# Holding GpSimd's indirect DMAs back so that at most two are queued

## The reference

```python
h = layernorm(x)
agg_in  = segment_mean((h @ W_in.T  + b_in )[src], dst)
agg_out = segment_mean((h @ W_out.T + b_out)[dst], src)
gi = concat([agg_in, agg_out]) @ W_ih.T + b_ih
gh = h @ W_hh.T + b_hh
r = sigmoid(i_r + h_r);  z = sigmoid(i_i + h_i)
n = tanh(i_n + r * h_n)
x = x + (1 - z) * h + z * n
f = layernorm(x)
p = softmax(relu(f @ router_w1 + router_b1) @ router_w2 + router_b2)
top_w, top_i = top_k(p, 2);  w = softmax(top_w)
x = x + sum(w * expert_out[top_i])      # 6 experts of three 256x256 layers
```

## Time and profile before

| | us |
|---|---|
| timed runs, median of 3 (lowest to highest) | 3107.05 (3097.07 to 3108.61) |
| the profiled execution: its span | 4434.5 |
| first scatter of GpSimd starts at | 114.68 |
| first gather of direction 0 starts at | 940.15 |
| first gather of direction 1 starts at | 2302.12 |
| first gather of the experts starts at | 4035.59 |

### The profile page before, as it was taken

How to read it: one execution, slowest core, us unless ns; L and a number is a source line. 1 busy time by engine, 2 the same in 40 slices (tenths; PEclk the granted TensorE clock), 3 DMA queues, 4 the chain that set the end, 5 groups by cost and what they waited for, 6 DMA issues and landing times. The chain is left out here.

```text
span 4434.5 us, 68226 instructions
## 1 busy us (share of the span) xinstructions
PE 2745.1 (62%) x14312; PEld 1616.8 (36%) x14313; DVE 2093.1 (47%) x6910; ACT 908.1 (20%) x1572; POOL 2164.5 (49%) x2165
## 2 busy tenths in 40 slices
PE   5211159977777777777764555555555555566896
PEld 2100025533333333333322333333333333345775
DVE  8201179975565556655552333443333433354221
ACT  4100026631112111111110010110111101112443
POOL 0777700035665555655645444444444444433786
PEclk9655589988888888888877777777777777787998
DMA  3100000022222222222222222222222222212444
GB/s 116 30 24 24 18 16 0 0 95 80 86 81 82 78 79 81 79 83 81 84 72 83 77 82 72 74 79 74 83 72 76 75 75 82 71 60 45 80 80 61
DMA packets 178175, 298.24 MB, mean 67 GB/s; under 512 B 51779, under 2 KB 123460, under 8 KB 178118
## 3 DMA queue, kind: packets, MB, share of 16 engines
q0 software_dynamic: 106560, 234.06, 19.8%
q10 hardware_dynamic: 44790, 35.90, 2.6%
q1 hardware_dynamic: 26768, 27.70, 2.0%
HBM read 255.56 MB, written 41.94 MB: 67 GB/s over the span
## 5 line engine op out<-in xcount | busy, mean ns | idle before, releaser
L431 POOL DMA_INDIRECT ring<-split_rows,live x782 | 791.5, 1012 | 923.4 <-DVE live L1035 381.8
L431 POOL DMA_INDIRECT over<-split_rows,gather_row x782 | 747.5, 956 | 933.0 <-PE bank L1674 681.5
L1600 PE MATMUL bank<-over,over 128*128 (+1 forms) x4920 | 1008.9, 354 | 143.1 <-issue 123.6
L1600 PEld LDWEIGHTS bank<-over,over 128*128 (+1 forms) x4920 | 485.9, 102 | 597.7 <-issue 351.9
L974 DVE TENSOR_SCALAR over<-iota_cols,live,live 128x128 f16 x1564 | 411.4, 319 | 119.9 <-issue 113.1
L392 POOL DMA_INDIRECT list<-sort,sort x336 | 332.7, 990 | 218.3 <-issue 111.0
L1674 PE MATMUL bank<-ring,dense 128*128 x980 | 329.5, 430 | 126.7 <-issue 100.1
L1714 PE MATMUL bank<-dense,dense 128*128 128x512 f32 (+1 forms) x600 | 262.0, 437 | 184.5 <-DVE dense L1183 174.1
L1675 PE MATMUL bank<-ones_col,dense 128*128 128x1 f16 x1960 | 334.9, 171 | 2.7 <-issue 2.5
L1674 PE MATMUL bank<-over,dense 128*128 x980 | 277.7, 386 | 94.5 <-issue 77.8
L614 ACT ACTIVATE over<-live,live 128x788 f16 x245 | 221.6, 945 | 492.2 <-remote 271.7
(11 more groups left out here) (304 smaller groups left out, 3927.7 us busy)
## 6 DMA issues: line engine op xcount, KB each, us to landing
norm<-in_x SPq DMA_DIRECT2D x20, 640.0 KB
ring<-split_rows,live POOLq DMA_INDIRECT x782
over<-split_rows,gather_row POOLq DMA_INDIRECT x782
split_rows<-over SPq DMA_DIRECT2D x10, 640.0 KB
in_edge_means<-dense ACTq DMA_DIRECT2D x50, 128.0 KB
dense<-in_x ACTq DMA_DIRECT2D x50, 128.0 KB
dense<-in_edge_means ACTq DMA_DIRECT2D x50, 128.0 KB
out<-dense ACTq DMA_DIRECT2D x25, 256.0 KB
```

Of the source, the lines that this page charges most:

```text
L431: g.indirect_dma_start(out=rings[d][:, i % ring_slots[d], :], out_offset=None, in_=table[:], in_offset=bass.IndirectOffsetOnAxis(ap=gather ...
L1600: ins = t.matmul(bank[h][:, 0:HS + 1], rows_(half), slots(h), start=False, stop=False, skip_group_check=True)
```

## The change

Ahead of each of the 2,116 indirect DMAs GpSimd's program gets a wait, and each of these DMAs gets a second semaphore, `sent`, which is raised when the DMA has left the engine (not when its rows have landed; the semaphores for that stay as they are). The wait ahead of the n-th DMA asks that `sent` stands at n - 2, so that at any time two indirect DMAs at most are with the engine. Nothing else is touched.

```diff
+SENT_AHEAD = 2
...
-        names = ("consts const_step spread_ready ...
+        names = ("sent consts const_step spread_ready ...
...
         @block.gpsimd
         def _(pool):
             g = nc.gpsimd
+            issued = [0]
+
+            def few_queued():
+                issued[0] += 1
+                if issued[0] > SENT_AHEAD:
+                    pool.wait_ge(S["sent"], issued[0] - SENT_AHEAD)
...
             for t_ in range(SORTED_TILES, NS):
+                few_queued()
                 g.indirect_dma_start(
                     out=lists[0][:], out_offset=bass.IndirectOffsetOnAxis(ap=list_at[:, t_:t_ + 1], axis=0),
-                    in_=payload[:, 0, t_:t_ + 1], in_offset=None,
+                    in_=payload[:, 0, t_:t_ + 1], in_offset=None, engine_sem=S["sent"],
                 ).then_inc(scatter_landed, 16)
...
                     if i % BATCH == 0 and i >= ring_slots[d]:
                         pool.wait_ge(S["slot_done"], d * NS + i + BATCH - ring_slots[d])
+                    few_queued()
                     g.indirect_dma_start(
                         out=rings[d][:, i % ring_slots[d], :], out_offset=None, in_=table[:],
                         in_offset=bass.IndirectOffsetOnAxis(ap=gather_row[d][:, i:i + 1], axis=0),
+                        engine_sem=S["sent"],
                     ).then_inc(ring_landed[d][i // BATCH % (ring_slots[d] // BATCH)], 16)
```

More of the change, by code:

```diff
@@ L297, in gnn_moe_program @@
         place_at = sb("place_at", [P, 2, 4], F32)
-        names = ("consts const_step spread_ready edges_in ln_mean ln_stats rows_scaled h_ready hi_ready split_ready table_stored "
+        names = ("sent consts const_step spread_ready edges_in ln_mean ln_stats rows_scaled h_ready hi_ready split_ready table_stored "
                  "dve_step onehot_ready onehot_used slots16_ready slot_prefix_ready base_ready "
```

## The result

The median of 20 timed runs after the change is 3114.80 us, of 20 runs before it 3102.32; the ratio, with one execution left out (below), is 1.0033, with a 95% interval of 1.0020 to 1.0046. The change costs some 10 us of 3100: within the half per cent that the prediction called no change and within its range, but clear of zero, and on the other side of zero than its 3105 (3107 - 2).

What follows compares the result with a forecast made beforehand. GpSimd's stream of indirect DMAs was taken as the bound. Median 3107 less a gain of 2, with wait, instructions and queued work at cost 0, gave 3105 us; range of this case 3085 to 3125, whole range 2990 to 3190.

Steps and rivals of the forecast that it cites:

- The stream is the bound: GpSimd's indirect DMAs, 1.25 to 1.32 us a step, already pace the timed runs; nothing else binds.
- chain without late signals: Whole kernel: GpSimd's scatters, gathers of both directions, stretches between and experts sum to 3082 us, timed median 25 above.
- TensorE was further from binding than feared: Gather stages: TensorE's 992 and 890 us lie under the stream's 1026 and 982, only 34 to spare in direction 0.
- Late signals a property of the profiled execution almost alone: TensorE's semaphores: lateness makes up the profile's 1353 us excess over 3082, hardly any of it in timed runs.
- "Cost 0" of the wait, with DMA n-1 as cover: Ahead of each indirect DMA: the 0.27 us release hides behind DMA n-1 with 0.98 us to spare; cost 0.
- The range of that term: Wait ahead of the 2,116 DMAs: bounds 0 and 571 us, the upper with DMAs served one at a time.
- The added instructions: A wait and semaphore more per DMA: bounds 0 and 127 us, taken as 0 from gathers already carrying a `slot_done` wait.
- A, the hold does nothing: Rival: queue not the cause, or `sent` raised on handing over; profile near 4430, timed 3107 us; chance 0.17.
- B, late signals in timed runs: Rival, faster: timed steps 0.82 us, TensorE binds after the change; 2919 us, or 3000 with half the lateness; chance 0.20.
- C, slower: Rival: hold not hidden, `sent` late or some ns per DMA; 10 ns make +21 us, 60 ns +127; chance 0.23.
- The gain of 2 us: Timed runs: of at most 25 us that the median has above the chain, the change removes 2.

Runs made afterwards that it cites:

- one execution left out (below): One of the 20 timed executions of the changed kernel, no further edit: 4257.33 us at a mean granted TensorE clock of 0.735.
- the earlier trace: The unchanged kernel as profiled ahead of the prediction: 4434.5 us at a mean granted TensorE clock of 0.808.

## Why the prediction was right and wrong

**The stream is the bound: right.** The prediction's chain without late signals came to 3082 us; the trace of the kernel before, taken again, spans 3092.5, that of the change 3100.1. Stage by stage, prediction and kernel before again: first gather 566 and 573.8, direction 0 1026 and 1021.4, direction 1 982 and 1010.4, experts' first gather 2683 and 2690.4. Of these, only direction 1 is off by more than 10 us: its gathers took 956 ns on average in the earlier trace rows and 986 here, which is 24 us. The stretches between the directions and ahead of the experts give 11 and 12 back (17.5 us for 28.8, 67 for 79), so that the total comes within 0.3% is in part luck. TensorE was further from binding than feared: 834 us in direction 0, not 992, with a granted clock of 0.98 there and not 0.85; the kernel before, taken again, has 837 us at 0.98.

**"Late signals a property of the profiled execution almost alone": right about timed runs, wrong about what they belong to.** The kernel before, profiled again, has none. The prediction saw that 4434.5 and 3107 do not belong together, and drew the right consequence, that the timed runs had nothing to give back. It took the wrong cause, and so credited the change with emptying the profile of "remote" waits and bringing the span to 3080 to 3200. The span did come to 3100.1, and the waits are gone, but the unchanged kernel does the same. Whether the hold would shorten an execution like that of the earlier trace rows is open, as no trace shows one with the hold.

**"Cost 0" of the wait, with DMA n-1 as cover: the step that failed.** As far as it went, it was right: `sent` comes 0.010 us after a DMA's end, the cover of 0.98 us is there, and the gathers start 0.30 us after the one before as ever, all but the 14 and the one behind the memsets; even one ahead costs a gather with a single wait nothing. What it did not ask is what else the long queue had covered. GpSimd's program itself stands still at 16 fixed gathers, so that with two waits the gather follows the end that `sent` tells of by 3.28 or 2.91 us (3.42 at gather 3), and with two DMAs handed over 14 of these standstills reach the engine: 8.8 us by the gaps, 10 us timed, where the prediction has 0. The prediction named the work that hides the wait, not the work that hid GpSimd's program. The gathers of the kernel before could not show the standstills, since with the queue full they leave no mark; the held kernels show them, by their fixed places, their fixed length and the 1.25 us that a further DMA takes off each. What the program does in them was not found.

**The range of that term.** 0 to 571 us for the release held the 10 us. The upper end was out of reach by another error: one at a time costs 220, not 571, since the release runs beside the 0.30 us and costs only the gathers with two waits.

**The added instructions: right at 0 in themselves.** The semaphore alone and three ahead both leave the gaps at 0.30. But the row that the prediction took the 0 from, a gather with the wait for its slot, has one wait, and the change gives each such gather a second. The separate instruction that this makes is where the program is stopped: with one wait a gather, or the two in the other order, the gaps fall from 8.8 to 1.1 us.

**The rivals.** A, the hold does nothing: half of it was so, as the emptied profile is none of its doing; but `sent` is not raised on handing over. The Trainium skill, page "Perfetto Trace Analysis", section "DMA Instruction — SWDGE (GPSIMD)", leaves open who would raise a further semaphore of such a DMA; the rise 0.010 us after the end of each DMA says that here it goes with the end of the DMA on the engine, and the held gathers say that the hold bites. B, late signals in timed runs: false, the steps of 1.25 us stand in the trace whose 3092.5 us are those of the timed runs. C, slower, has the sign, 0.23 by the prediction, but not the mechanism: `sent` is not late, and a cost of some ns for each DMA is ruled out by the scatters, whose gaps sum to 107.5 us with and without the hold, and by three ahead, where no gap is left.

**The gain of 2 us: not there.** The chain had left 25 us between itself and the median, and the prediction gave the change a share of it. The kernel before, traced again, has no late signal to remove.

## What to carry to other kernels

When the profiled execution and the timed median don't agree, look first at the granted clock and profile the kernel again before explaining its waits: of the 4434.5 us here, 1342 were the execution's, not the kernel's. A queue in front of an engine covers not only the engine's waits but also the lateness of the program that fills it, and that lateness shows only when the queue is shortened; so ask of each hold how far ahead the program must be, and try one place more. A second wait on an instruction can stop the program ahead of it: of two waits, let the separate one be the one that is nearly always met (by the gaps here, 1.1 us in place of 8.8; the timed ratios, 1.0015 and 1.0033, are too near to tell).

## What had not been expected of the hardware

- The standstills of GpSimd's program stand at fixed gathers, 104 apart with a ring of 16 slots and 88 apart with 32, with 1.25 or 2 instructions of the program for a gather (and, in direction 0, with 1), and are longer by 0.37 us with the ring of 16 (2.03 and 1.66 us, two waits, two ahead). What makes them was not found.
- The scatters have two fixed gaps of their own, ahead of scatters 113 and 226, in every trace. They do not hang on the hold (3.00 us at 113 with two and with eight ahead, 2.99 with one, 3.02 with none), so a longer queue does not cover them as it covers those of the gathers. In the kernel before, where they are 6.0 of the 111.0 us of "issue" in the earlier trace rows, and in the change:

```profile
264.54 0.97 POOL L392 DMA_INDIRECT list<-sort,sort  x1 [3.02 <-issue]
...
270.14 1.13 POOL L401 DMA_INDIRECT list<-sort,sort  x1 [3.00 <-issue]
```

- With one DMA ahead, a single wait for the end of the DMA before adds nothing to the 0.30 us between two DMAs; as a separate instruction, it makes 0.75 us of the 0.30.
- In the execution of the earlier trace rows, TensorE's signals came late, as in the 11.5 us of the earlier trace rows, and waits of up to 21.0 us ended with them. They lie between 142 us and the end of direction 1, where GpSimd has its long streams of indirect DMAs, with a granted clock of 0.85 and 0.77 in the two directions in place of 0.98 and 0.92. What causes such an execution stays open.
